# Layer two of a gated attention and feed-forward block: high and low parts as one moving operand

## The reference

```
x = x + tanh(g_xattn) * attention(layernorm(x), ctx)      # 16 heads of 32
h = concat([layernorm(x), -layernorm(x)])
h = relu(s0 * (h @ W0)) * 2         # 1024 -> 2048, weights are +1 or -1
h = relu(s1 * (h @ W1)) * 2         # 2048 -> 2048, weights are +1 or -1   <- layer two
x = x + tanh(g_ffn) * s2 * (h @ W2) # 2048 -> 512
```

## Time and profile before

| | |
|---|---|
| median of 3 runs | 1603.56 us (1602.43 to 1603.7) |
| the profiled execution's own time | 1602.88 us |
| its span, first to last instruction | 1601.1 us |
| TensorE busy | 1525.5 us, 95% |
| VectorE busy | 942.0 us, 59% |
| ScalarE busy | 674.0 us, 42% |
| mean granted TensorE clock | 0.986 of full speed |

### The profile page before, as it was taken

One profiled execution on the slowest core, in us unless ns is written; L12 is line 12 of the kernel. 1 busy time (PEld: TensorE's weight loads), 2 busy tenths in 40 slices (PEclk: granted clock), 3 DMA queues, 4 the chain that ended last, 5 costly groups with the idle time before them and its releaser, 6 DMA issues.

```text
span 1601.1 us, 46093 instructions
## 1 busy us (share of the span) xinstructions
PE 1525.5 (95%) x19856; PEld 1297.7 (81%) x19856; DVE 942.0 (59%) x1924; ACT 674.0 (42%) x1568; POOL 168.8 (11%) x275
## 2 busy tenths in 40 slices
PE   5549999999999999999999999999999999999998
PEld 3428778888888888888888889888888988889887
DVE  6729865664656566565656656565655656565442
ACT  2414244352635435263544525354452535445231
POOL 4000101001010100102010010202001020201100
PEclk9779999999999999999999999999999999999999
DMA  7252315243332424343252433324243432424100
GB/s 239 50 119 66 68 52 90 58 98 66 85 70 60 89 59 97 64 88 74 58 98 47 99 61 94 68 63 98 45 98 61 94 67 67 94 49 99 28 28 14
DMA packets 278226, 120.95 MB, mean 76 GB/s; under 512 B 243464, under 2 KB 259848, under 8 KB 277896
## 3 DMA queue, kind: packets, MB, share of 16 engines
q1 hardware_dynamic: 275960, 117.48, 33.9%
q10 hardware_dynamic: 2064, 0.53, 0.1%
HBM read 37.76 MB, written 16.78 MB: 34 GB/s over the span
## 4 chain that ended last, share of the span: by engine, by line
PE 79%; DVE 9%; ACT 4%; DMA 3%; issue 2%; SPq 1%; POOL 0%; DVEq 0%; ACTq 0%; POOLq 0%
PE bank L1215 19%; PE bank L1216 19%; PE bank L1182 7%; PE bank L1183 7%; PE bank L1232 6%; PE bank L1233 6%; ACT Pf L513 2%; PE bank L1100 2%; PE bank L1101 2%; PE bank L1102 2%; PE bank L1084 2%; DVE nmax L787 2%; PE bank L1086 2%; PE bank L1085 2%; DMA PT<-Phl 1%
## 5 line engine op out<-in xcount | busy, mean ns | idle before, releaser
L1215 PE MATMUL bank<-H,W 128*128 128x128 f16 x6720 | 778.3, 219 | 5.1 <-ACT C L606 4.0
L1216 PE MATMUL bank<-H,W 128*128 128x128 f16 x6720 | 778.0, 219 | 0.0
L1215 PEld LDWEIGHTS bank<-H,W 128*128 128x128 fp8e5 x6720 | 655.4, 98 | 17.3 <-ACT C L606 9.7
L1216 PEld LDWEIGHTS bank<-H,W 128*128 128x128 fp8e5 x6720 | 657.4, 98 | 7.1
L1182 PE MATMUL bank<-hT,W 128*128 128x256 f16 x1024 | 227.2, 273 | 3.3 <-DVE hT L729 1.7
L1183 PE MATMUL bank<-hT,W 128*128 128x256 f16 x1024 | 227.1, 273 | 0.0
L513 ACT ACTIVATE Pf<-bank,nmax 128x128 f32<-128x128 f32 x512 | 146.3, 368 | 143.5 <-DVE nmax L787 134.6
L1232 PE MATMUL bank<-W,h 128*128 128x512 fp8e5 x512 | 194.0, 379 | 1.6 <-DVE h L835 1.6
L1233 PE MATMUL bank<-W,h 128*128 128x512 fp8e5 x512 | 194.0, 379 | 0.0
L462 POOL TENSOR_TENSOR attn<-pvs 128x128 f32<-128x128 f32 x120 | 75.4, 629 | 1024.9 <-DVE pvs L800 1024.9
L827 DVE TENSOR_TENSOR C<-bank,C 128x256 f32<-128x256 f32 x180 | 76.2, 423 | 162.4 <-ACT C L606 89.9
(11 more groups left out here) (128 smaller groups left out, 1890.8 us busy)
## 6 DMA issues: line engine op xcount, KB each, us to landing
Qst<-q_bounce SPq DMA_DIRECT2D x120, 128.0 KB, 2.7
Y<-in_x_dram SPq DMA_DIRECT2D x16, 512.0 KB, 3.8
R<-X SPq DMA_DIRECT2D x16, 512.0 KB, 3.5
q_bounce<-Qhl SPq DMA_DIRECT2D x120, 64.0 KB
out_dram<-R SPq DMA_DIRECT2D x15, 512.0 KB, 2.6
W<-in_L_ffn_k_dram SPq DMA_DIRECT2D x8, 512.0 KB, 8.0
PT<-Phl SPq DMA_TRANSPOSE x120, 3.1
H<-in_L_xattn_Wk_dram SPq DMA_DIRECT2D x1, 1024.0 KB, 9.7
```

The lines of the kernel that those rows point to most:

```text
L1215: mm(o, w, H0[:, 0, i, b_of, :], start=first, stop=False, skip_group_check=True)
L1216: last = mm(o, w, H0[:, 1, i, b_of, :], start=False, stop=i == PAIRS - 1, skip_group_check=True)
```

## The change

A product of layer two now takes 16 matmuls of 256 moving columns: one load of the weights, then the high part's 128 columns and the low part's 128 columns as one moving operand. The two parts land in different columns of the bank, so a bank holds for each output tile a high sum and a low sum of 128 columns, and fills all 512 columns. The sums are joined outside TensorE. `parts_of(bank, hl)` is the view of one part. `add_low` adds the low sum of A to the tile after ScalarE copied the high one. `add` becomes two additions in sequence. P4 no longer goes right from the bank: its high sum is copied to C11, its low sum is added on VectorE, and relu and the rest read C11; both stand in the slot of P3. TensorE waits for `l1_low` (the low sum is added) where it waited for `l1_copy`, and also before P1.

```diff
@@ ScalarE @@
             def take(q, s, f, to, bank):
                 act.wait_ge(l1_done, nth(f, NL1, 7 * q + s))
-                nc.scalar.activation(to[:, :, :], banks[bank][:, 0:CHUNK].rearrange("p (j n) -> p j n", j=2),
-                                     ACT.Copy).then_inc(l1_copy, 1)
+                nc.scalar.activation(to[:, :, :], parts_of(banks[bank], 0), ACT.Copy).then_inc(l1_copy, 1)
...
                     if s == P1:
+                        if n > 0:
+                            act.wait_ge(h1_lo, nth(f, NH, 4 * (n - 1) + 2))
+                        elif f >= 2:
+                            act.wait_ge(h1_lo, nth(f - 1, NH, 4 * GROUPS - 2))
                         take(n, s, f, C11, A)
...
                     if s == P4:
-                        act.wait_ge(l1_done, nth(f, NL1, 7 * n + s))
-                        nc.scalar.activation(h1_part(n, 1, 1, 0),
-                                             banks[A][:, 0:CHUNK].rearrange("p (j n) -> p j n", j=2), ACT.Relu)\
-                            .then_inc(h1_hi, 1)
+                        act.wait_ge(h1_lo, nth(f, NH, 4 * n))
+                        take(n, s, f, C11, A)
                     if s == P3:
+                        act.wait_ge(l1_low, nth(f - 1, NA, 4 * n + 3))
+                        nc.scalar.activation(h1_part(n, 1, 1, 0), C11[:, :, :], ACT.Relu).then_inc(h1_hi, 1)
@@ VectorE @@
+        def parts_of(bank, hl):
+            return bank[:, :].rearrange("p (j a n) -> p a j n", j=2, a=2)[:, hl]
...
+            def add_low(q, s, f, to, copy):
+                dve.wait_ge(l1_copy, nth(f - 1, NA, 4 * q + copy))
+                V_.tensor_tensor(to[:, :, :], parts_of(banks[A], 1), to[:, :, :], ALU.add).then_inc(l1_low, 1)
+            def add(q, s, f, to, bank, low, n):
+                dve.wait_ge(l1_low, nth(f - 1, NA, 4 * q + low))
                 dve.wait_ge(l1_done, nth(f, NL1, 7 * q + s))
-                V_.tensor_tensor(to[:, :, :], banks[bank][:, 0:CHUNK].rearrange("p (j n) -> p j n", j=2),
-                                 to[:, :, :], ALU.add).then_inc(l1_sum, 1)
+                V_.tensor_tensor(to[:, :, :], parts_of(banks[bank], 0), to[:, :, :], ALU.add).then_inc(l1_half, 1)
+                dve.wait_ge(l1_half, nth(f - 1, NC, 3 * q + n))
+                V_.tensor_tensor(to[:, :, :], parts_of(banks[bank], 1), to[:, :, :], ALU.add).then_inc(l1_sum, 1)
...
+                    if s == P1:
+                        add_low(n, s, f, C11, 0)
                     if s == P2:
-                        dve.wait_ge(l1_copy, nth(f - 1, NC, 3 * n))
-                        add(n, s, f, C11, B)
+                        add(n, s, f, C11, B, 0, 0)
                     if s == P6:
                         h1_rest(n, 0, f, 0, 1, C11[:, :, :])
+                        add_low(n, s, f, C12, 1)
                     if s == P7:
-                        add(n, s, f, C22, C)
+                        add_low(n, s, f, C22, 2)
+                        add(n, s, f, C22, C, 2, 1)
                         h1_rest(n, 1, f, 1, 0, C22[:, :, :])
                     if s == P4:
-                        h1_rest(n, 2, f, 1, 1, banks[A][:, 0:CHUNK].rearrange("p (j n) -> p j n", j=2))
+                        add_low(n, s, f, C11, 3)
                     if s == P3:
-                        add(n, s, f, C12, C)
+                        h1_rest(n, 2, f, 1, 1, C11[:, :, :])
+                        add(n, s, f, C12, C, 1, 2)
                         h1_rest(n, 3, f, 0, 0, C12[:, :, :])
@@ TensorE @@
                     if n < 2 and f >= 2:
-                        pe.wait_ge(h1_lo, nth(f - 1, NH, NH - 2))
+                        pe.wait_ge(l1_low, nth(f - 2, NA, NA - 1))
...
                     if s == P1 and n > 0:
-                        pe.wait_ge(h1_lo, nth(f, NH, 4 * (n - 1) + 2))
+                        pe.wait_ge(l1_low, nth(f - 1, NA, 4 * (n - 1) + 3))
                     if s == P6:
-                        pe.wait_ge(l1_copy, nth(f - 1, NC, 3 * n))
+                        pe.wait_ge(l1_low, nth(f - 1, NA, 4 * n))
                     if s == P7:
-                        pe.wait_ge(l1_copy, nth(f - 1, NC, 3 * n + 1))
+                        pe.wait_ge(l1_low, nth(f - 1, NA, 4 * n + 1))
                     if s == P4:
-                        pe.wait_ge(l1_copy, nth(f - 1, NC, 3 * n + 2))
+                        pe.wait_ge(l1_low, nth(f - 1, NA, 4 * n + 2))
...
                         for j in range(2):
-                            o = banks[bank][:, j * HALF:(j + 1) * HALF]
                             w = W1[:, n, a_of, i, j * P:(j + 1) * P]
-                            first = opens and i == 0 and j == 0
-                            mm(o, w, H0[:, 0, i, b_of, :], start=first, stop=False, skip_group_check=True)
-                            last = mm(o, w, H0[:, 1, i, b_of, :], start=False, stop=i == PAIRS - 1,
+                            last = mm(banks[bank][:, j * CHUNK:(j + 1) * CHUNK], w, H0[:, :, i, b_of, :],
+                                      start=opens and i == 0 and j == 0, stop=i == PAIRS - 1,
                                       skip_group_check=True)
```

More of the change, by code:

```diff
@@ L249, in gated_block_kernel @@
             "l0_done", "l0_relu", "l0_step", "l0_t", "l0_hi", "l0_lo"))
-        l1_done, l1_copy, l1_sum, h1_hi, h1_lo = (sem(n) for n in (
-            "l1_done", "l1_copy", "l1_sum", "h1_hi", "h1_lo"))
+        l1_done, l1_copy, l1_low, l1_half, l1_sum, h1_hi, h1_lo = (sem(n) for n in (
+            "l1_done", "l1_copy", "l1_low", "l1_half", "l1_sum", "h1_hi", "h1_lo"))
         l2_done, l2_last, out_ready = sem("l2_done"), sem("l2_last"), sem("out_ready")
         NU, NT, NG, NX = U, TT, G, 3 * TT
-        NP, NL1, NC, NH, NL2 = PAIRS, 7 * GROUPS, 3 * GROUPS, 4 * GROUPS, 2 * GROUPS
+        NP, NL1, NC, NA, NH, NL2 = PAIRS, 7 * GROUPS, 3 * GROUPS, 4 * GROUPS, 4 * GROUPS, 2 * GROUPS
         CUT = {"T1": 0, "CT": TT, "T2": 2 * TT}
@@ L823, in pair_lo @@
                     .then_inc(l0_lo, 1)
-            def add(q, s, f, to, bank):
+            def add_low(q, s, f, to, copy):
[3 more added lines that the diff above has]
+                dve.wait_ge(l1_low, nth(f - 1, NA, 4 * q + low))
                 dve.wait_ge(l1_done, nth(f, NL1, 7 * q + s))
-                V_.tensor_tensor(to[:, :, :], banks[bank][:, 0:CHUNK].rearrange("p (j n) -> p j n", j=2),
-                                 to[:, :, :], ALU.add).then_inc(l1_sum, 1)
+                V_.tensor_tensor(to[:, :, :], parts_of(banks[bank], 0), to[:, :, :], ALU.add).then_inc(l1_half, 1)
+                dve.wait_ge(l1_half, nth(f - 1, NC, 3 * q + n))
+                V_.tensor_tensor(to[:, :, :], parts_of(banks[bank], 1), to[:, :, :], ALU.add).then_inc(l1_sum, 1)
             def h1_part(q, half, late, hl):
@@ L869, in feed @@
                 if kind == "L1":
+                    if s == P1:
+                        add_low(n, s, f, C11, 0)
                     if s == P2:
-                        dve.wait_ge(l1_copy, nth(f - 1, NC, 3 * n))
-                        add(n, s, f, C11, B)
+                        add(n, s, f, C11, B, 0, 0)
                     if s == P6:
                         h1_rest(n, 0, f, 0, 1, C11[:, :, :])
+                        add_low(n, s, f, C12, 1)
                     if s == P7:
-                        dve.wait_ge(l1_copy, nth(f - 1, NC, 3 * n + 2))
-                        add(n, s, f, C22, C)
+                        add_low(n, s, f, C22, 2)
+                        add(n, s, f, C22, C, 2, 1)
                         h1_rest(n, 1, f, 1, 0, C22[:, :, :])
                     if s == P4:
-                        h1_rest(n, 2, f, 1, 1, banks[A][:, 0:CHUNK].rearrange("p (j n) -> p j n", j=2))
+                        add_low(n, s, f, C11, 3)
                     if s == P3:
-                        dve.wait_ge(l1_copy, nth(f - 1, NC, 3 * n + 1))
-                        add(n, s, f, C12, C)
+                        h1_rest(n, 2, f, 1, 1, C11[:, :, :])
+                        add(n, s, f, C12, C, 1, 2)
                         h1_rest(n, 3, f, 0, 0, C12[:, :, :])
```

## The result

| | before | after |
|---|---|---|
| median | 1603.12 us (1602.43 to 1603.7, 4 runs) | 1670.48 us (1667.68 to 1671.66, 4 runs) |
| span of the profiled execution | 1601.1 us | 1669.9 us |
| ratio after / before | | 1.042, 95% interval 1.0404 to 1.0435 |

The forecast was 1664 us, range 1632 to 1696. The time grew by 67.4 us where 60.4 were worked out.

A forecast was written before the change was run, and what follows sets the result against it. TensorE was taken as bound by its own matmul pace. Per chunk, new waits +5.51 less pace 1.18 gave +4.33; times 14 +60.7, chunk 15 -0.7, end +0.4: +60.4, so 1664 us, range 1632 to 1696.

The forecast's parts named there:

- The pace: Layer two's matmuls: 109.1 ns per 256 columns against 111.6 ns per pair of 128, 17 us gained, 1.18 us per chunk.
- The bad end: Layer two's moving operand: the jump between its two runs costs another fixed 2.5 ns per matmul, +17 us, no gain left.
- The hand-overs and gaps: Layer two, one chunk: TensorE waits for copy and addition in sequence; starts between engines 0.03 to 0.27 us apart, from rows.
- all six gaps: P4 of q0 1.37; P1, P6, P7 of q1 0.35, 1.74, 0.49; P1, P6 of q2 0.23, 1.96 us.
- The sum per chunk: Layer two's gaps in one chunk total 6.14 us; less 0.63 before and 1.18 of pace, +4.33.
- One chunk times 14: Chunks 1 to 14, with woven attention, taken as alike: 14 x 4.33 = +60.7 us.
- The late transposes: Ahead of PV5: transposed probabilities may come late, some 0.2 us per chunk more, outside the sum.
- Chunk 15 and the end: Chunk 15, without woven attention: -0.7 us; the kernel's end, one addition more: +0.4 us.
- the ring: q0 to q2: ScalarE's copy behind exponentials, behind VectorE's maximum, behind additions; four more VectorE instructions there make P6 of q1 wait 1.74.
- the chain's time: Ahead of layer two's matmuls: TensorE idle 85 to 90 us, nearly all by VectorE's addition of a low sum.
- the clock: Rival: each of three large gaps per chunk brings a clock fall of 1.3 us, 55 us, 1719 us; chance 0.03.

## Why the prediction was right

- **The pace**, worked out as 17.5 us from layer one's rows: 16.6 alone. (The row read for it gives 1.78 / 32 = 55.6 ns, not 55.8; over all products the distance is 55.8.) The bad end, +17 for the operand of two runs, didn't come.
- **The hand-overs and gaps.** In the chunk that is shown all six gaps came where they were put, in the order of size that was worked out, five of six within 0.1 us. The sum per chunk was 6.14, it is 6.54 there. That term was 0.4 short; measured, 0.26 of it is GpSimd's hindrance, which moved P6 of q1 from 1.71 to 1.97, and 0.17 small errors at P4 of q0 and P6 of q2.
- **One chunk times 14.** The chunks are less alike than the sum took them. In the profiled executions layer two of the 14 chunks takes 983.9 us before and 1049.3 after: 4.67 a chunk, not the 4.84 of the chunk that is shown, for 4.33 worked out. That is 65.4 us for 60.7, so 4.7 us of what is missing. The late transposes, which the prediction named as a bound of 0.2 us per chunk and left out of the sum, are a part of it; where they come ahead of P6 of q2 they eat into its gap, so their price can't be read by itself.
- **Chunk 15 and the end.** Here -0.3 us was worked out, and it is +1.5 (71.7 for 70.2 from the start of layer two of chunk 15). The sum had no term for the fall of the clock at the end: seven distances of the matmuls that follow the idle time are 0.43 us instead of 0.21, and two are 0.32, 1.7 us in all. Another 1.7 us lie ahead of layer two of chunk 1, where no part of the change runs; why is not shown. With layer two's 65.4 that is nearly all of the 68.8 us by which the two spans differ; the medians differ by 67.4.
- **What it rests on.** The prediction took the ring from the rows of before: a copy behind exponentials, behind a maximum, behind additions. The order on ScalarE alone gave 46 of the 84 us back, and one instruction that TensorE doesn't wait for ahead of P6 grew that gap by 0.47. Of the other 38 us no experiment shows how much is queueing.
- **Wrong beside it.** It said that the chain's time would show as 85 to 90 us of idle time; the page prints 70.5, since it counts from the modelled end of the last matmul. Of the rivals, the clock, at 0.03, was closer than it looked: no fall in layer two of the changed kernel after idle stretches of up to 1.90 us, but one at the end after 2.04, and one in every chunk as soon as one more instruction made the stretch 2.27. Each of those costs some 1.6 us, where 1.3 was read from the start of the kernel.

## What to carry to other kernels

Work out where an added instruction stands in the queues of the engines that wait for each other, not its busy time: here 168 us more of VectorE's time, on an engine that was 59% busy, cost 84 us of TensorE's, and order alone returned 46. A wait is off such a ring only if the instruction that ends it is, too: moved from VectorE's addition to ScalarE's copy, the wait ahead of P6 of q1 grew, since that copy stood behind VectorE's maximum. What a reordered or delayed item issues, its DMA too, becomes late next. And a chunk that is worked out in full still has to be checked against the others before it is multiplied.

## What the runs showed of the hardware

- TensorE's clock: matmuls of 256 columns follow each other at 109 ns at 2.4 GHz and at about 213 at 1.2 GHz. In layer two of the changed kernel, with idle stretches of up to 1.90 us, it did not fall; at the kernel's end it fell once, after 2.04. With the copy of both sums it fell after 3 of 13 stretches of 2.02 to 2.03 us, with one more instruction after each of 14 of 2.20 to 2.28 us (a window with the fall has a mean of 0.69), and with the stretched table on the kernel before once after 1.96. But the 2.18 us at the end of the kernel with the copy of both sums brought none.
- VectorE and GpSimd: an instruction of VectorE that reads and writes SBUF took 680 ns instead of 425 where it started 0.45 us into GpSimd's addition of 128x128, and 420 when that was moved. Where it started before that addition it kept 420 to 430. VectorE's maximum and additions out of PSUM showed no such loss.
- PSUM filled to 512 columns by each product, read in runs of 128: a copy still takes 0.38 us and an addition 0.42.
